# A graph network stack: the first stage's PReLU regrouped so that it starts in PSUM, its normalisation moved to GpSimd, its product given a PSUM bank of its own

## The reference

```
x = layernorm(x + prelu(adj @ (x @ W0) + bias0, a))            # L0
x = layernorm(x + adj @ (x @ W1) + bias1)                      # L1
x = layernorm(x + GRU, 5 layers: m = h @ W[l];                 # L2
              agg = (adj != 0)^T @ m; h = gru_cell(agg, h))
x = layernorm(x + sum of 5 small graph convolutions on         # L3
              subsets of the first 25 nodes)
```

## Time and profile before

| | |
|---|---|
| median of 3 runs | 1041.41 us (1040.25 to 1042.65) |
| the profiled execution | 1039.74 us |
| its span | 1037.8 us |
| mean granted TensorE clock | 0.986 |
| TensorE busy | 968.0 us, 93% |
| VectorE busy | 888.4 us, 86% |
| ScalarE busy | 774.0 us, 75% |
| GpSimd busy | 755.1 us, 73% |

### The profile page before, as it was taken

One profiled execution on the slowest core, in us unless ns is written; L12 is line 12 of the kernel. 1 busy time (PEld: TensorE's weight loads), 2 busy tenths in 40 slices (PEclk: granted clock), 3 DMA queues, 4 the chain that ended last, 5 costly groups with the idle time before them and its releaser, 6 DMA issues.

```text
span 1037.8 us, 19369 instructions
## 1 busy us (share of the span) xinstructions
PE 968.0 (93%) x6010; PEld 580.8 (56%) x6010; DVE 888.4 (86%) x2190; ACT 774.0 (75%) x1319; POOL 755.1 (73%) x853
## 2 busy tenths in 40 slices
PE   6989999999999999999999999999899999989894
PEld 5855555555555555555555555555454444558783
DVE  6988889999988999899989998899888977964555
ACT  3768777787878787877878787878788887875552
POOL 2665667788887898889787888678788996975201
PEclk8989999999999999999999999999999999999997
DMA  5443336342654346423754366434633475440121
GB/s 162 114 92 84 70 82 123 73 82 62 123 115 88 66 90 116 93 61 71 130 108 82 62 113 122 80 72 95 123 72 57 82 139 85 69 97 21 33 59 31
DMA packets 295338, 90.72 MB, mean 87 GB/s; under 512 B 222447, under 2 KB 295108, under 8 KB 295236
## 3 DMA queue, kind: packets, MB, share of 16 engines
q1 hardware_dynamic: 295236, 89.49, 43.3%
HBM read 28.67 MB, written 8.81 MB: 36 GB/s over the span
## 4 chain that ended last, share of the span: by engine, by line
PE 47%; DVE 24%; issue 11%; ACT 11%; POOL 3%; SPq 1%; DMA 1%; DVEq 0%; POOLq 0%; ACTq 0%
PE psum L1509 10%; PE psum L1514 10%; PE psum L1510 10%; PE psum L1433 7%; PE psum L1541 3%; DVE n L1233 3%; DVE shared L1299 3%; DVE shared L1285 3%; DVE shared L1292 2%; PE psum L1589 2%; DVE shared L1311 2%; PE psum L1622 2%; ACT shared L908 2%; DVE psum L1273 2%; DVE x3q L983 1%
## 5 line engine op out<-in xcount | busy, mean ns | idle before, releaser
L723 POOL TENSOR_TENSOR shared<-shared 128x512 f32<-128x512 f32 x160 | 206.4, 1290 | 42.1 <-ACT shared L937 41.9
L677 POOL TENSOR_TENSOR shared<-shared 128x512 f16<-128x512 f32 x128 | 150.5, 1176 | 85.9 <-ACT shared L890 85.2
L1509 PE MATMUL psum<-shared,wh_hi 128*128 128x512 f16 x480 | 183.0, 381 | 32.0 <-ACT shared L937 14.7
L1514 PE MATMUL psum<-shared,wx_hi 128*128 128x512 f16 x480 | 182.1, 379 | 1.6 <-DVE shared L1311 1.5
L1514 PE MATMUL psum<-shared,wh_hi 128*128 128x512 f16 x480 | 182.1, 379 | 0.0
L1510 PE MATMUL psum<-shared,wh_lo 128*128 128x512 f16 x480 | 182.1, 379 | 0.0
L1509 PE MATMUL psum<-shared,wx_hi 128*128 128x512 f16 x480 | 181.9, 379 | 0.0
L1510 PE MATMUL psum<-shared,wx_lo 128*128 128x512 f16 x480 | 181.9, 379 | 0.0
L879 ACT ACTIVATE psum<-shared,nbn,nunscale 128x512 f32<-128x512 f32 x160 | 124.9, 781 | 63.3 <-DVE shared L1299 62.5
L1285 DVE SCALAR_TENSOR_TENSOR shared<-psum,bhn,shared 128x512 f32<-128x512 f32 x160 | 118.4, 740 | 42.5 <-ACT shared L908 41.4
L908 ACT ACTIVATE shared<-psum,brz,unscale 128x512 f32<-128x512 f32 x160 | 123.9, 774 | 29.2 <-PE psum L1514 27.5
(11 more groups left out here) (187 smaller groups left out, 1839.2 us busy)
## 6 DMA issues: line engine op xcount, KB each, us to landing
m<-in_adj_dram SPq DMA_DIRECT2D x32, 256.0 KB, 3.3
m<-in_x_dram SPq DMA_DIRECT2D x32, 256.0 KB, 3.7
adjr<-in_adj_dram SPq DMA_DIRECT2D x32, 256.0 KB, 3.1
out_dram<-x SPq DMA_DIRECT2D x8, 768.0 KB
shared<-shared SPq DMA_TRANSPOSE x192, 3.1
out_dram<-shared SPq DMA_DIRECT2D x32, 50.0 KB
v<-in_L_gnn_W_dram SPq DMA_DIRECT2D x10, 128.0 KB, 2.4
x3q<-x SPq DMA_DIRECT2D x16, 50.0 KB
```

Source lines behind the costliest of these rows:

```text
L677: nc.gpsimd.tensor_tensor(HT_LO[s % 2], HT[s][:, :], HT_HI[s % 2], ALU.subtract).then_inc(b_htl, 1)
L723: nc.gpsimd.tensor_tensor(ZH[s % 2][:, :], ZW[s % 2][:, :], HT[s][:, :], ALU.mult).then_inc(b_zh, 1)
L1509: mm(dst, w_h[:, col:col + P], h[:, :], start=start, stop=False)
L1514: return mm(dst, w_h[:, col:col + P], lo[:, :], start=False, stop=stop)
```

## The change

- L0's result is grouped in another way: x + prelu(z) = (x + a*z) + (1-a)*relu(z). VectorE computes WS0 = z*a + X0 straight from PSUM (`sloped`, part 2), ScalarE replaces z by relu(z) in the same bank (part 2), VectorE adds: WS0 = relu(z)*(1-a) + WS0 (`bent`, part 4). The tiles UP and UN, one Relu per step and GpSimd's addition are gone.
- The four applies of L0's normalisation go from VectorE (parts 3 and 4) to GpSimd (`apply_x1`, part 2).
- z must stay in its bank from part 1 to part 4: it has bank 5 alone, and the other parts share bank 4 (bank 7 for part 0 of step 8). The waits of TensorE follow that.
- In the steps alone the same three changes; ScalarE's Relu goes behind the copy of the transposed adjacency. `bent` stands behind `second_sum` in VectorE's queue, and TensorE's next z waits for `bent`.
- The first two adjacency tiles of stage B are loaded two `load_a` earlier and converted one step earlier (`first_adjacency`, before `first_x`).
- `normalised` runs in part 3 from slot 23 instead of part 2 from slot 22.
- Two waits for `a_x2` are added ahead of L917 and L922, on the engine that gives that signal itself.

```diff
         def a_bank(part, k):
-            return bank[4 + ((k - ALONE) * PIECES + part) % 2]
+            return bank[5] if part == 1 else bank[7] if part == 0 and k == ALONE else bank[4]
...
-            for k in range(4, ALONE):
+            for k in range(4, ALONE - 2):
                 load_a(k)
             for s in range(2):
                 load_b(s, 0)
+            for k in range(ALONE - 2, ALONE):
+                load_a(k)
...
+            def apply_x1(k, m, p):
+                pool.wait_ge(a_rs0, k - 1)
+                for i in range(G4):
+                    last = nc.gpsimd.tensor_scalar(cols(X1[(m - 2) % 4], i), cols(WS0[p], i),
+                                                   MV0[p][:, 2 * i:2 * i + 1], RS0[p][:, i:i + 1],
+                                                   ALU.subtract, ALU.mult)
+                last.then_inc(a_x1, 1)
...
-                if part == 2 and has(1):
-                    pool.wait_ge(a_up, k)
-                    pool.wait_ge(a_x1, k - 2)
-                    nc.gpsimd.tensor_tensor(WS0[(m - 1) % 2][:, :], UP[:, :], X0[(m - 1) % 4][:, :], ALU.add)\
-                      .then_inc(a_xu, 1)
+                if part == 2 and has(2):
+                    apply_x1(k, m, p)
...
-                if part == 1 and has(1):
-                    act.wait_ge(a_z0, k)
-                    act.wait_ge(a_xu, k - 1)
-                    nc.scalar.activation(UP[:, :], a_bank(1, k)[:, :], ACT.Relu).then_inc(a_up, 1)
-                    act.wait_ge(a_w0, k - 1)
-                    nc.scalar.activation(UN[:, :], a_bank(1, k)[:, :], ACT.Relu, scale=-1.0).then_inc(a_un, 1)
+                if part == 2 and has(1):
+                    act.wait_ge(a_xu, k)
+                    nc.scalar.activation(a_bank(1, k)[:, :], a_bank(1, k)[:, :], ACT.Relu).then_inc(a_up, 1)
...
+            def sloped(k, m, z):
+                dve.wait_ge(a_z0, k)
+                if k >= 3:
+                    dve.wait_ge(a_x1, k - 2)
+                nc.vector.scalar_tensor_tensor(WS0[(m - 1) % 2][:, :], z[:, :], alpha[:, 0:1],
+                                               X0[(m - 1) % 4][:, :], ALU.mult, ALU.add).then_inc(a_xu, 1)
+
+            def bent(k, m, u):
+                dve.wait_ge(a_up, k)
+                dve.wait_ge(w_bias, 7)
+                nc.vector.scalar_tensor_tensor(WS0[(m - 1) % 2][:, :], u[:, :], rest[:, 0:1],
+                                               WS0[(m - 1) % 2][:, :], ALU.mult, ALU.add).then_inc(a_w0, 1)
...
             def step_a(k, m, has):
                 if has(1):
-                    dve.wait_ge(a_un, k)
-                    dve.wait_ge(a_xu, k)
-                    nc.vector.scalar_tensor_tensor(WS0[(m - 1) % 2][:, :], UN[:, :], nalpha[:, 0:1],
-                                                   WS0[(m - 1) % 2][:, :], ALU.mult, ALU.add).then_inc(a_w0, 1)
-                if has(2):
-                    p = m % 2
-                    apply(lambda i: cols(X1[(m - 2) % 4], i), WS0[p], MV0[p], RS0[p], G4, a_rs0, k - 1, a_x1)
+                    sloped(k, m, bank[2])
                 if has(3):
+                    second_sum(k, m, bank[4])
                 if has(1):
+                    bent(k, m, bank[2])
                     norm(WS0[p], ST0, MV0[p], G4, a_w0, k, a_bs0, a_mv0)
...
             def piece_a(part, k, m, has):
+                if part == 2 and has(1):
+                    sloped(k, m, a_bank(1, k))
                 if part == 3 and has(3):
+                    second_sum(k, m, a_bank(2, k))
-                if part >= 3 and has(2):
-                    p = m % 2
-                    dve.wait_ge(a_rs0, k - 1)
-                    for i in (0, 1) if part == 3 else (2, 3):
-                        last = nc.vector.tensor_scalar(cols(X1[(m - 2) % 4], i), cols(WS0[p], i),
-                                                       MV0[p][:, 2 * i:2 * i + 1], RS0[p][:, i:i + 1],
-                                                       ALU.subtract, ALU.mult)
-                    if part == 4:
-                        last.then_inc(a_x1, 1)
                 if part == 4 and has(1):
-                    dve.wait_ge(a_un, k)
-                    dve.wait_ge(a_xu, k)
-                    nc.vector.scalar_tensor_tensor(WS0[(m - 1) % 2][:, :], UN[:, :], nalpha[:, 0:1],
-                                                   WS0[(m - 1) % 2][:, :], ALU.mult, ALU.add).then_inc(a_w0, 1)
+                    bent(k, m, a_bank(1, k))
...
                 if part == 0 and has(3):
                     pe.wait_ge(a_x1, k - 2)
-                    if k == ALONE:
+                    if has(1):
+                        pe.wait_ge(a_yT0, k)
+                    else:
                         pe.wait_ge(a_w1, k - 3)
-                    if not has(1):
-                        pe.wait_ge(a_un, STEPS_A)
-                        pe.wait_ge(a_w1, k - 4)
                 if part == 1 and has(1):
                     pe.wait_ge(a_yT0, k)
+                    pe.wait_ge(a_w0, k - 1)
                 if part == 3 and has(0):
-                    pe.wait_ge(a_un, k)
+                    pe.wait_ge(a_w1, k - 2)
                 if part == 4 and has(0):
                     pe.wait_ge(a_adjT, k + 1)
-                    pe.wait_ge(a_w1, k - 2)
...
-L3_FROM, L3_DEG, L3_AN, L3_POWS = 22, 6, 12, 14
+L3_FROM, L3_DEG, L3_AN, L3_POWS = 23, 6, 12, 14
```

87 lines of the change are left out of this document (36 added, 51 removed).

## The result

The changed kernel takes 1030.58 us (median of four runs, 1029.57 to 1030.70) against 1041.43 for the kernel before in the same session: a ratio of 0.9905, 95% interval 0.9888 to 0.9923. It is faster by 1.0%, where 2.6% was forecast. It lies 8.6 us above the forecast's own range (1006 to 1022) and 1.6 above the wider one that took in the rivals (1001 to 1029). Its profiled execution has a span of 1027.8 us against 1037.8.

The account below looks back on a forecast made before the run. TensorE's 104.4 us bounds a 112.7 us round, the rest waiting, mostly for VectorE, slowed by GpSimd. Rounds -26.3, other slots -4.7, bursts +2, normalised +2.5, start -1: -27.5, from 1039.74 to 1012.2, median 1014, range 1006 to 1022.

Parts of the forecast that it names:

- the floor: TensorE's own work in a round of twenty slots, without waits: 104.4 us, against 112.7 a round taken.
- The Z waits: TensorE's waits in the rounds for ScalarE's Z sigmoid: 3.0 us a round, forecast to stay.
- Slots 5 to 19 and 120 to 139: Slots outside the five full rounds, taken to wait at about half the rounds' rate: -4.7 us.
- The first stage alone: Eight steps before the slots: TensorE's new wait for `bent` eats existing idle time; zero, between -2 and +4 us.
- the 1.4 in hand: GpSimd's slack before slot 0's P products; 0.8 us delay lands there once a round, booked 0.3 a round, 2 in all.
- the 5.3 a round: TensorE's waiting in each full round put down to VectorE and ScalarE's R sigmoid; its removal gives -26.3 us over five rounds.
- (a): Rival, rounds: ScalarE's order decides more slots, Z waits grow and half the gain is lost: 1029 us; chance 0.14.
- (c): Rival, rounds: GpSimd's applies now hold up VectorE's remaining SBUF-to-SBUF work, +14 us: 1028; chance 0.08.
- (b): Rival, rounds: Z waits shrink too since ScalarE starts slots earlier, 10.5 us less: 1003; chance 0.11.
- (e): Rival, rounds: VectorE's time falls but the span does not, TensorE's gaps being its own: about 1041 us; chance 0.03.
- (d): Rival, rounds: GpSimd becomes the bound, from 1.46 us a tensor_scalar; at 1.6, +15 us: 1057; chance 0.03.
- by the start alone: Rival, start: slower there (clock lost), with no gain in the rounds; no size given; chance 0.03.

Follow-up runs that it names:

- the old steps alone: Changed kernel with its eight steps alone worked as in the kernel before, pieces, bank and earlier adjacency staying changed: 1014.18 us, ratio 0.9772.
- the broadcast kernel: Changed pieces behind the old steps alone, GpSimd's four applies replaced by two 128x512 tensor_tensor with broadcast mean and scale: 1015.96 us, ratio 0.9775.

## Why the prediction was wrong

**Right: what bounded the rounds.** The waits for VectorE went altogether, part-4 slots fell (the fifth of a round from 7.23 to 5.36), and slots without a wait take 5.22, 5.44, 5.44, 4.86: the 104.4 of the floor within 0.1 a slot. The Z waits stayed (12.0 us before, 10.5 now); moving ScalarE's work did not remove them but shifted them. Slots 5 to 19 and 120 to 139 gave 3.5 of 4.7. The applies back on VectorE show that taking the applies out of the collision with GpSimd is worth 2.2 a round, the rest of the change 1.4. With the old steps alone the change reaches a ratio of 0.9772, near the 0.974 of the forecast. That nearness is in part luck: the 2.5 us booked for `normalised` were not spent and hide part of what GpSimd and the floor were mis-sized by, and 1.8 us come from the first R pass, no more than it differs between executions.

**The step that failed: "The first stage alone ... Zero, between -2 and +4".** The first R pass came 12.5 us later; against the old steps in the same slots 14.2. I followed one new wait, TensorE's for `bent`, and asked what would cover it. I did not go through ScalarE's queue in the same way: the moved Relu waits for `sloped`, and behind it stand the YT1 copy and the x2 applies. For the pieces in the slots I had made exactly that argument and found nobody late. The same window of the kernel before and of the changed kernel (PE, PEld, DVE, ACT, POOL; then the granted clock, DMA share and GB/s):

```profile
35.00:55.00 20.00, 16.52 (x124) 14.69 (x123) 19.38 (x82) 16.66 (x38) 14.18 (x24) 0.97 0.58 126
```

```profile
35.00:55.00 20.00, 15.55 (x99) 12.50 (x98) 12.19 (x49) 9.54 (x20) 15.27 (x25) 0.91 0.33 72
```

Before, VectorE was busy for 19.38 of 20 us: any wait added to its ring lengthens these steps, and that could have been read before the forecast. After, it is busy for 12.19 only. It has less to do and stands in the ring: `sloped` comes behind two norms (2.5 us together), whatever stands behind its reader on ScalarE is late with it, and `second_sum` and the norms wait for that. That the first stage had 3.09 us of idle TensorE as a cushion was true and no help, since VectorE had hardly any. Shown by edits are the 14.2 us (the old steps take them away) and the 8.8 of them that the Relu's place in the queue cost; the other 5.4 are argued.

**Mis-sized: GpSimd.** The piece was booked at 0.53 from the memset, with an upper bound of 0.73; it takes 0.80. Both neighbours were wrong ones: memset reads nothing, and I took the two-input tensor_tensor for an upper rate (2.5 ns a column), while two operations of tensor_scalar cost 3.4. So the burst is 3.2 us instead of 2.1, and the 1.4 in hand in front of slot 0's P products is gone: 1.15 a round (6.46 against 5.31 in slot 0), where 0.3 was booked. In slots 20 to 119 this came four times, 4.6 us, where 2 was booked for the whole kernel. My own condition for this was written down ("if the P products begin to wait for the transposes").
The Trainium skill ("GPSIMD Engine Reference", section 4.1), by which a one-input operation runs roughly at line rate, does not agree with these rows: 1.51 us for one operation on 512 columns, more than the 1.28 of a two-input product of the same size (L725).

**Mis-sized: the floor.** Five slots without a wait take 5.22 + 5.44 + 5.44 + 4.86 + 5.31 = 26.27, a round 105.1 and not 104.4. So 0.7 of the 5.3 a round that were put down to VectorE and the R sigmoid were no wait and could not go: 3.5 us in five rounds. With it and the 4.6 the 26.3 of the forecast become 18.2; 17.9 was measured.

**Small terms.** `normalised`: booked 2.5, not to be seen. The adjacency tiles: booked -1, not to be seen. Slots 5 to 19 and 120 to 139: 35/20 x 5.3 x 0.5 is 4.6, where the sum has 4.7. Of the +1.6 after slot 140, 1.45 is slot 149 alone (5.78 against 4.33), in which the P products wait 1.27 for a transpose; why, and where the -1.7 in the last stage comes from, was not followed up.

**The rivals.** Neither (a) nor (c) came: R waits are 0.3 us, and no wait of TensorE for VectorE is left. (b) came at most in small: the Z waits fell by 1.5 us. (e) is out, since the rounds fell by 3.6. (d), the GpSimd rival, named the right engine with the wrong form: it is not the bound of the round (183.6 of 200) but late once a round, in the one place where it had 1.4 in hand. The slower rival "by the start alone" named the right place at 0.03; its effect came together with the gain.

The Trainium skill's caution ("Perfetto Trace Analysis", Optimizing Scalar/DVE Operations), that moving work between VectorE and GpSimd might not help, held for this change only in part: the full move gives 2.2 a round, and moving half of it gives 0.6 more than that, since the other engine's queue has deadlines of its own.

## What to carry to other kernels

When an edit moves an instruction or gives it a new wait, read in every stage of the kernel what stands behind it in its queue and whether its releaser is on an engine with no time to spare there; a move that is free in the steady state can close a ring in the stage ahead of it. Before moving work to another engine, price its form (operations, pointer scalars, inputs) and its burst against the tightest deadline of that queue, not against the engine's mean load; splitting the work over both engines may beat either. Here the changed slots behind the old steps alone, with the applies shared two and two, take 1009.7 us.

## What the runs showed of the hardware that I had not expected

- GpSimd's tensor_scalar on 128x512 fp32: 1.51 us with one operation, 1.95 with two, 2.08 with two pointer scalars. Its two-input tensor_tensor takes 1.28, and 1.05 to 1.08 for 128x512 with a broadcast operand (the means of the two lines of the broadcast kernel): as two such instructions the applies take 2.1 us, as four tensor_scalar pieces 3.2.
- Pointer scalars cost GpSimd 0.156 us on a 128x128 instruction (0.799 against 0.643).
- VectorE's scalar_tensor_tensor with one input in PSUM was never stretched (0.745 mean and at most 0.753 in the changed kernel), also directly behind tensor_scalar instructions from SBUF to SBUF that GpSimd stretched to 1.47 and 1.97 a pair.
- Thirteen small copies of VectorE from SBUF to SBUF took 1.26 us beside GpSimd's tensor_scalar pieces and 3.89 beside its tensor_tensor with a broadcast operand and the one behind it, in the same slot (28).
- TensorE's granted clock over the first 80 us differs from execution to execution of the same steps (0.84 or 0.91 to 1.00 in the same stretch), with 1.8 us between their first R passes. Whether the clock makes that difference is not shown: what follows in the slots differs too.
